# Main attention of a two-layer block: square turns on VectorE, 32-row products of the values in two pieces, each head weighed by itself

## The chip, the cores and the metric

One core of a Trainium2 chip runs the whole program in one launch. The metric is device time in microseconds (us). All matrix work runs on the TensorE into PSUM, which has eight banks of 128 partitions x 512 float32. VectorE (DVE in the rows), ScalarE (ACT) and GpSimd (POOL) do the rest, and SyncE (SP) issues most DMAs.

## The reference, cut to what matters

Two transformer layers over 1024 tokens of width 256. The change lies in the first layer's main attention: 16 heads, queries and keys of 192 columns (128 plain, 64 rotated), values that come from 64 latent columns.

```
qf = concat([q_nope, q_pe], -1);  kf = concat([k_nope, k_pe], -1)
scores = einsum('bhqd,bhkd->bhqk', qf, kf) * scale
probs  = softmax(scores)                    # 1024 x 1024 for each of 16 heads
ctx    = einsum('bhqk,bhkd->bhqd', probs, v)
main_out = ctx @ o_w.T
out = gates[..., 0:1] * main_out + gates[..., 1:2] * pattern_out
```

Beside it stand a second ("pattern") attention, whose stage comes first, a mixture of experts, and in the second layer a causal attention and another mixture of experts. They are not touched.

## The kernel before, in words

The weights are folded so that a head's keys and queries are 128 columns wide (64 latent, 64 rotated) and the values of all heads are the same 64 latent columns `kvx`; the head's value and output weights are folded into `mo` (256 columns for each pair of heads).

Main attention is cut into 32 units. Unit u is a pair of heads (u // 4) and 256 queries (u % 4), and has four score blocks i of 128 queries x 1024 keys: head i % 2, query half i // 2. One block takes these steps:

- `pe_score` (L1850 to L1852): six TensorE products of 512 columns (three split products for each half of the keys) into one of two bank pairs, `wide[0]` and `wide[1]` (banks 0 to 3). The two pairs alternate, so block n waits for the exponential of block n - 2.
- `dve_score` (L1859): VectorE takes the negated row maximum of 1024 columns.
- `act_expo` (L1874): ScalarE takes the exponential into `Pq`, of which there are eight, with the row sums as an accumulator.

The values need the keys on the partitions. `pe_transposed` (L1883) turns the four blocks of a unit with TensorE, four 128x128 squares into one bank for each of eight key tiles k; `act_copy` (L1896) copies six of the eight tiles to SBUF and `dve_copy` (L1901) the two in `BY_VECTOR`. `pe_pvm` (L1951) then makes the products of the values: for each k and each head one of 128 rows (keys), 64 weight columns and 256 moving columns. Head 0 goes to partitions 0 to 63 of bank 6, head 1 to 64 to 127.

Meanwhile `dve_recip` takes the reciprocals of the row sums, times the gate, and turns them in a small square turn (L1917); `sp_shares` and `sp_spread` carry them by DMA through HBM to `Rs`. `dve_weigh` (L1962) multiplies bank 6 by `Rs` into `OTm` in one operation, `pe_project_out` (L1974) multiplies by `mo`, and `dve_add_out` (L1988) adds to x.

Every pair's queries and keys are prepared beside the pair before it: `pe_prep` (L1604; six products, four `rope` and two `lat`), `act_product` (L1637, the copy), `sp_swap` (four DMAs that swap halves for the rotation) and `pool_product` (L1659 to L1685, GpSimd: cosine, sine, sum, cast, subtraction). The copy of product k waits for the swap and the cosine product of k - 1, or for its low part when that one was a `lat`.

The order of work is written out by hand in `main_order`; every engine runs its own steps of that list in order. In unit u stand the scores and exponentials of unit u + 1, the eight turns of unit u with their copies, and the values, weighing, projection and addition of unit u - 1. One preparation product stands every fifth turn. The banks 4, 5 and 7 go around among turns, projections and preparation products (`PTB`).

Of the kernel before, what the change touches and what calls it, by code (L numbers as in the profile page):

```python
# [62 lines left out]
PREP_EVERY = 5  # L63

BY_VECTOR = (0, 6)


def up(x, half, m):
# [6 lines left out]
    (28, 7): [("temperature",), ("wup", 0), ("wdown", 0)],  # L75
    (30, 6): [("stats", 0)],
    (31, 2): [("normed", 0)],
    (31, 5): [("turn", 0), ("hT", 0)],
    (31, 7): [("wup", 1), ("wdown", 1)],
    (31, "values"): [("logits", 0)],  # L80
}


def main_order():

    order = [("expo", 0, 1), ("score", 0, 2), ("score", 0, 3), ("ctx", 0), ("ctx", 1), ("expo", 0, 2), ("cadd", 0),  # L90
             ("ctx", 2), ("expo", 0, 3), ("cadd", 1), ("ctx", 3), ("cadd", 2), ("cadd", 3)]
    chunks = []

    def turn(u, k):
        order.extend([("t", u, k), ("copy", u, k)])
        if chunks:
            order.extend(chunks.pop(0))
        order.extend(BESIDE_LAST.get((u, k), ()))

    def score(u, i):  # L100
        if u < 32:
            order.append(("score", u, i))

    def expo(u, i):
        if u < 32:
            order.append(("expo", u, i))

    def output(u):
        order.extend([("project", u), ("add", u)])

    for u in range(32):
        if u % 4 == 0 and u // 4 + 1 < 8:
            for i in range(len(FIRST)):
                chunks.extend([[("prep", u // 4 + 1, i), ("pcopy", u // 4 + 1, i)]] + [[]] * (PREP_EVERY - 1))
        score(u + 1, 0)
        turn(u, 0)
        order.append(("rec", u))
        score(u + 1, 1)
        expo(u + 1, 0)
        turn(u, 1)  # L120
        if u:
            order.extend([("pv", u - 1), ("ot", u - 1)])
        expo(u + 1, 1)
        turn(u, 2)
        score(u + 1, 2)
        turn(u, 3)
        if u:
            output(u - 1)
        expo(u + 1, 2)
        turn(u, 4)  # L130
        order.append(("spread", u))
        score(u + 1, 3)
        turn(u, 5)
        turn(u, 6)
        expo(u + 1, 3)
        turn(u, 7)
    assert not chunks
    order.extend([("pv", 31)] + BESIDE_LAST[31, "values"] + [("ot", 31)])
    output(31)
    return order  # L140

# [196 lines left out]
def program(nc, a, out):  # L338
# [27 lines left out]
    bank = [wide[i // 2][:, i % 2, :] for i in range(4)] + [nc.alloc_psum_tensor(f"bank{i}", [128, 512], F32)[:] for i in range(4, 8)]  # L366
# [128 lines left out]
    Pq = [MP.sb("Pq0", [128, T], F32)]  # L495
    Pt = [sb("Pt0", [128, 512], F32, at=W0A), sb("Pt1", [128, 512], F32, at=HN)]
    M1 = Region(S0 + 64 * 1024)
    Pq += [M1.sb(f"Pq{i}", [128, T], F32) for i in range(1, 7)]
    Pt += [M1.sb("Pt2", [128, 512], F32), MP.sb("Pt3", [128, 512], F32)]
    M1 = Region(HTP)  # L500
    Pq += [M1.sb("Pq7", [128, T], F32)]
    Pt += [M1.sb(f"Pt{i}", [128, 512], F32) for i in range(4, 10)]
    Pql = Pq[:7] + [sb("Pq7l", [128, T], F32, at=WKPE + 4096)]
    Ptl = Pt[:4] + [sb(f"Pt{i}l", [128, 512], F32, at=(KV + 2048 * (i - 4) if i < 8 else WKPE + 2048 * (i - 8)))
                    for i in range(4, 10)]
# [736 lines left out]
    mp_ok, tr_mm, ev_v, clear_ok = (sem(n) for n in ("mp_ok", "tr_mm", "ev_v", "clear_ok"))  # L1242
# [383 lines left out]
    def act_product(e, p, k):  # L1626
# [10 lines left out]
        e.activation(t12[:, 0, :], bank[PTB["prep", p, k][0] if p else BANK_P0[k][0]][:], ACT.Copy).then_inc(pc_ok, 1)  # L1637
# [156 lines left out]
    pta_ok, ptv_ok = sem("pta_ok"), sem("ptv_ok")  # L1794
    d_shares, d_spread = sem("d_shares"), sem("d_spread")
    for s_ in MAIN:
        if s_[0] == "score":
            slot_ = s_[2] % 2 if s_[1] == 0 else 1 - s_[2] % 2
# [3 lines left out]
    PTB, PTC = {}, {}  # L1802
    free_, copies_ = [(cadd_ok, 3), (op_cT, 4), (cadd_ok, 4)], [0, 0]
    for s_ in MAIN:
        if s_[0] in ("t", "project", "prep"):
            b_ = len(PTB) % 3
            PTB[s_] = ((4, 5, 7)[b_], free_[b_])
            if s_[0] == "project":
                free_[b_] = (add_ok, s_[1] + 1)
            elif s_[0] == "prep":  # L1810
                free_[b_] = (pc_ok, len(FIRST) * s_[1] + s_[2] + 1)
            else:
                v_ = s_[2] in BY_VECTOR
                copies_[v_] += 1
                PTC[s_[1:]] = ((pta_ok, ptv_ok)[v_], copies_[v_])
                free_[b_] = PTC[s_[1:]]
# [5 lines left out]
    def probabilities(u, i):  # L1822
        n = 4 * u + i
        return (Pql if u >= 30 else Pq)[n % 8]
# [1476 lines left out]
```

## Time and profile before

| | |
|---|---|
| time, median of 3 runs | 1294.52 us (1292.11 to 1296.56) |
| the profiled execution | 1291.33 us, its span 1289.5 us |
| busy share of the span | PE 96%, DVE 60%, ACT 57%, POOL 41% |
| mean granted TensorE clock | 0.992 |
| turns on TensorE (L1883) | 1024 of 128x128 |
| products of the values (L1951) | 512, in 1024 records |

In the profile a float32 product leaves two records, so that one unit's sixteen products of the values show as x32; a turn, and a product of the split type, leaves one. The duration of a record on PE holds its way through the array, so records that follow each other overlap; what a product costs is the distance from start to start. PEld is the load of the weights, which runs beside the products. The main attention runs from about 265 us to about 770 us of the span.

### The profile page before, as it was taken

What the parts mean: (1) busy time and instruction counts of PE and PEld (TensorE: products, weight loads), DVE (VectorE), ACT (ScalarE), POOL (GpSimd) and SP (SyncE); (2) the same over time, 40 slices, a digit from 0 to 9 for tenths busy, and PEclk for the clock granted to TensorE, in tenths of its full rate; (3) what the DMA queues carried; (4) which work ended last, traced back from release to release, by engine and by line L of the source; (5) the groups of instructions that cost most, each with busy time, mean ns of one, the idle gap of its engine ahead of it and who ended that gap; (6) DMA issues with size and microseconds to landing.
All of it is one profiled execution on the core that took longest, in us unless ns stands there. A gap on an engine that the chain in (4) does not pass through costs nothing.

```text
span 1289.5 us, 22502 instructions
## 1 busy us (share of the span) xinstructions
PE 1243.0 (96%) x8298; PEld 875.0 (68%) x8298; DVE 768.3 (60%) x1254; ACT 732.9 (57%) x1370; POOL 533.4 (41%) x531
## 2 busy tenths in 40 slices
PE   8999999999999999999999998999998998999997
PEld 5544334477777777777777777889753444678997
DVE  4689978245454444445454666555667763855555
ACT  3479978855555555555555635332355676435553
POOL 5266274248576666767666124443100000512211
PEclk9999999999999999999999999999999999989999
DMA  7780000001101011111111021020233310101111
GB/s 287 200 180 2 2 19 11 10 18 29 38 22 38 22 38 27 32 32 32 29 36 54 25 72 76 27 72 12 74 74 88 72 38 1 34 17 33 50 42 34
DMA packets 40887, 64.44 MB, mean 50 GB/s; under 512 B 8221, under 2 KB 27421, under 8 KB 39837
## 3 DMA queue, kind: packets, MB, share of 16 engines
q1 hardware_dynamic: 40776, 62.99, 17.8%
q8 instruction: 67, 1.10, 0.4%
q14 instruction: 44, 0.35, 0.1%
HBM read 45.60 MB, written 8.45 MB: 42 GB/s over the span
## 4 chain that ended last, share of the span: by engine, by line
PE 85%; DVE 8%; ACT 3%; issue 2%; DMA 1%; POOL 1%; SPq 0%; ACTq 0%; DVEq 0%; POOLq 0%
PE bank L1951 9%; PE bank L1883 9%; PE bank L1513 8%; PE bank L2151 6%; PE bank L2152 6%; PE bank L2153 6%; PE bank L1604 5%; PE bank L1850 5%; PE bank L1852 5%; PE bank L1851 5%; PE bank L1470 4%; PE bank L1333 3%; PE bank L1974 2%; PE bank L1450 2%; DVE mpc L1412 2%
## 5 line engine op out<-in xcount | busy, mean ns | idle before, releaser
L1859 DVE TENSOR_REDUCE nmq<-bank 128x1 f32<-128x1024 f32 x128 | 155.8, 1217 | 151.8 <-PE bank L1852 151.8
L1491 ACT ACTIVATE Pb<-bank 128x512 f32<-128x512 f32 (+3 forms) x355 | 180.6, 573 | 30.2 <-PE bank L1470 9.3
L1896 ACT ACTIVATE Pt<-bank 128x512 f32<-128x512 f32 x187 | 110.7, 594 | 118.8 <-PE bank L1883 117.9
L1874 ACT ACTIVATE Pq<-bank,nmq 128x1024 f32<-128x1024 f32 x127 | 141.7, 1116 | 58.7 <-DVE nmq L1859 58.7
L1341 DVE TENSOR_REDUCE mp<-bank 128x2 f32<-128x1024 f32 x128 | 153.5, 1221 | 27.5 <-PE bank L1333 26.7
L1883 PE MATMUL bank<-idf,Pq 128*128 128x128 f32 x1016 | 145.7, 275 | 1.4 <-ACT Pq7l L1874 1.2
L1883 PEld LDWEIGHTS bank<-idf,Pq 128*128 128x128 f32 x1016 | 119.1, 140 | 36.5 <-issue 11.9
L1412 DVE TENSOR_REDUCE mpc<-bank 128x2 f32<-128x1024 f32 (+2 forms) x96 | 88.4, 953 | 46.3 <-PE bank L1400 23.2
L1951 PE MATMUL bank<-Pt,kvx 128*64 128x256 f32 x992 | 114.1, 382 | 0.0
L1850 PE MATMUL bank<-qk1h,qk0h 128*128 128x512 f32 x256 | 109.4, 427 | 0.4 <-ACT Pq L1874 0.4
L1513 PE MATMUL bank<-Pb,vx 128*17 128x256 f32 (+3 forms) x1222 | 106.3, 407 | 0.7 <-ACT OTa L1527 0.5
L1852 PE MATMUL bank<-qk1h,qk0l 128*128 128x512 f32 x256 | 100.8, 394 | 0.0
L1851 PE MATMUL bank<-qk1l,qk0h 128*128 128x512 f32 x256 | 100.0, 391 | 0.0
L1951 PEld LDWEIGHTS bank<-Pt,kvx 128*64 128x64 f32 x992 | 68.6, 137 | 37.7 <-issue 6.6
L2126 POOL TENSOR_TENSOR cTt<-cTt,gab 128x256 f32<-128x256 f32 x8 | 6.1, 760 | 181.9 <-DVE cTt L2121 181.6
L2353 POOL TENSOR_TENSOR hl<-hf,hh 128x512 fp32r<-128x512 f32 x32 | 41.8, 1307 | 83.8 <-ACT hh L2340 83.8
L1661 POOL TENSOR_TENSOR t<-t,sinT 128x512 f32<-128x512 f32 x32 | 40.9, 1278 | 74.7 <-DMA t<-t 74.5
L1470 PE MATMUL bank<-qstr,kstr 64*128 64x512 f32 x256 | 70.9, 494 | 0.6 <-ACT Pb L1491 0.6
L2567 POOL TENSOR_TENSOR v1l<-wr,v1h 128x512 fp32r<-128x512 f32 x25 | 32.1, 1288 | 95.0 <-ACT v1h L2562 95.0
L1470 PEld LDWEIGHTS bank<-qstr,kstr 64*128 64x128 f32 x256 | 28.2, 183 | 56.8 <-ACT Pb L1491 36.2
L1659 POOL TENSOR_TENSOR Rt<-t,cosT 128x512 f32<-128x512 f32 x32 | 41.1, 1285 | 60.0 <-ACT t L1637 58.5
L1450 PE MATMUL bank<-qst,kst 107*128 107x512 bf16 (+3 forms) x192 | 54.3, 333 | 7.8 <-ACT qst L1437 3.5
(374 smaller groups left out, 2951.7 us busy)
## 6 DMA issues: line engine op xcount, KB each, us to landing
t<-t SPq DMA_DIRECT2D x128, 64.0 KB, 2.0
wr<-wf SPq DMA_DIRECT2D x25, 256.0 KB, 2.6
wraw<-wf SPq DMA_DIRECT2D x8, 768.0 KB, 4.6
scratch<-stgr SPq DMA_DIRECT2D x4, 1024.0 KB, 4.0
Rs<-shares SPq DMA_DIRECT2D x64, 64.0 KB, 2.7
scratch<-stg SPq DMA_DIRECT2D x8, 384.0 KB, 2.6
qst<-scratch SPq DMA_DIRECT2D x9, 256.0 KB, 8.4
owT<-owT SPq DMA_DIRECT2D x1, 2048.0 KB, 11.2
```

Source lines behind the costliest of these rows:

```text
L1341: e.tensor_reduce(mp[:, w % 3, :, j, kh], wide[slot][:], AX, ALU.max).then_inc(ring_ok, 1)
L1412: e.tensor_reduce(mpc[:, w // 2 % 3, a0:a0 + 2, j, kh], wide[slot][:, :, 0:c], AX, ALU.max).then_inc(ring_ok, 1)
L1470: e.matmul(bank[b][:], kst2[r, hp, kt * 128:kt * 128 + 128], qst2[r, hp, cols(half)], start=True, stop=True).then_inc(st_mm[0], 1)
L1491: e.activation(PBR[l][i % len(PBR[l])][:, 0:c], bank[b][:, 0:c], ACT.Exp, scale=0.25).then_inc(exp_ok[0], 1)
L1513: last = e.matmul(bank[6][32 * a:32 * a + 17, to:to + c], vx[:, t, h * 17:h * 17 + 17], PBR[l][i % len(PBR[l])][:, q0:q0 + c], start=(t == ...
L1850: e.matmul(o, qh[:, qs], kh[:, ks], start=True, stop=False)
L1851: e.matmul(o, qh[:, qs], kl[:, ks], start=False, stop=False)
L1852: last = e.matmul(o, ql[:, qs], kh[:, ks], start=False, stop=True)
L1859: e.tensor_reduce(nmq[:, n % 8:n % 8 + 1], scores(u, i), AX, ALU.max, negate=True).then_inc(mp_ok, 1)
L1874: e.activation(probabilities(u, i)[:], scores(u, i), ACT.Exp, bias=nmq[:, n % 8:n % 8 + 1], accum_out=sums[:, u % 2, i:i + 1]).then_inc(ex ...
L1883: last = e.transpose(bank[b][:, 128 * c:128 * c + 128], probabilities(u, 2 * (c % 2) + c // 2)[:, 128 * k:128 * k + 128], idf[:])
L1951: last = e.matmul(bank[6][64 * hd:64 * hd + 64, 0:256], kvx[:, k, :], transposed(u, k)[:, 256 * hd:256 * hd + 256], start=(k < 1), stop=(k ...
```

## The change

- *Turns.* `pe_transposed`, `act_copy` and `dve_copy` are gone. `dve_turn` lets VectorE transpose one score block of 128x1024, in 32x32 squares, from one of three `P` buffers (before: eight `Pq`) into `PT[u % 2]`, a tile of 32 key blocks x 128 columns. After it, key 32 b + r of a query block stands at row r of the row group its queries were in: rows 32 g to 32 g + 31 of `PT` hold 32 keys for the queries of row group g, and the 128 columns are two query halves of two heads, 32 each. The exponential of block n waits for the turn of block n - 3.
- *Values.* `sp_values` lays the values out four times, once, with sixteen DMAs: `kv4[s]` has keys 32 s to 32 s + 31 of every 128 in each of the four row groups. `pe_pvm` makes 32 x 4 products of 32 rows, 64 weight columns and 128 moving columns, row group g into bank 4 + g, in two pieces of 16 key blocks: `("pv", u, 0)` and `("pv", u, 1)`. The four banks are one PSUM tensor `rest`.
- *Weighing.* `dve_weigh` runs once for each head, over partitions 0 to 63 of the four banks, and writes the head's half of `OTm`.
- *Banks.* The projection always goes to bank 7 and preparation products to 5 and 6 in turn, which the values use as well. So the values of a unit wait for the addition of the unit before and for ScalarE's copies of all preparation products ahead of them (`COPIED`), and a preparation product for the last weighing ahead of it and for the copy before the last.
- *Order.* `main_order` is written anew: in unit u the values of u - 1 stand in two pieces, after score blocks 2 and 3; the projection of u - 2 after score block 0; preparation products at places `PREP_AT`, counted in score blocks. The steps for the experts beside the last units stand at other places.

```diff
+PREP_AT = ((4, 5, 8, 9, 12, 13), (0, 1, 4, 8, 9, 12))
...
+    preps = {16 * (p - 1) + at: (p, i) for p in range(1, 8) for i, at in enumerate(PREP_AT[p > 1])}
...
+    for u in range(1, 32):
+        order.append(("score", u, 0))
+        output(u - 2)
+        prep(4 * u)
+        order.extend([("rec", u - 1), ("vturn", u - 1, 3), ("expo", u, 0)])
+        order.extend(BESIDE_LAST.get((u, 0), ()))
+        order.append(("score", u, 1))
+        prep(4 * u + 1)
+        order.extend([("spread", u - 1), ("vturn", u, 0), ("expo", u, 1)])
+        order.extend(BESIDE_LAST.get((u, 1), ()))
+        order.extend([("score", u, 2), ("pv", u - 1, 0), ("vturn", u, 1), ("expo", u, 2)])
+        order.extend([("score", u, 3), ("pv", u - 1, 1), ("ot", u - 1), ("expo", u, 3), ("vturn", u, 2)])
+    output(30)
+    order.extend([("rec", 31), ("vturn", 31, 3), ("turn", 0), ("spread", 31), ("pv", 31, 0), ("pv", 31, 1), ("hT", 0),
+                  ("wup", 1), ("wdown", 1), ("ot", 31), ("project", 31), ("logits", 0), ("add", 31)])
...
+    def dve_turn(e, u, i):
+
+        c, n = 64 * (i % 2) + 32 * (i // 2), 4 * u + i
+        e.wait_ge(exp_ok[1], n + 1)
+        if i == 0 and u >= 2:
+            e.wait_ge(pv_mm[1], u - 1)
+        elif i == 0:
+            e.wait_ge(*((pv_mm[0], 128), (op_mm, 4))[u])
+        source = probabilities(u, i)[:].rearrange("p (b k) -> p b k", k=32)
+        if u < 31:
+            e.transpose(PT[u % 2][:, :, c:c + 32], source).then_inc(pt_ok, 1)
...
+    def sp_values(e):
+
+        e.wait_ge(sh_mm, 16)
+        e.wait_ge(pv_mm[0], 128)
+        for s in range(4):
+            for g in range(4):
+                e.dma_start(kv4[s][32 * g:32 * g + 32, :, :], kvx[32 * s:32 * s + 32, :, :]).then_inc(d_kv, 16)
...
-    def pe_pvm(e, u):
...
-        for k in range(NT):
-            for hd in range(2):
-                last = e.matmul(bank[6][64 * hd:64 * hd + 64, 0:256], kvx[:, k, :],
-                                transposed(u, k)[:, 256 * hd:256 * hd + 256],
-                                start=(k < 1), stop=(k == NT - 1), skip_group_check=True)
-        last.then_inc(pv_mm[1], 1)
+    def pe_pvm(e, u, part):
+
+        if part == 0:
+            if u:
+                e.wait_ge(ot_ok[1], u)
+                e.wait_ge(add_ok, u)
...
+            e.wait_ge(*COPIED[u])
+            e.wait_ge(pt_ok, 4 * u + 4)
+        for b in range(16 * part, 16 * part + 16):
+            for g in range(4):
+                rows = slice(32 * g, 32 * g + 32)
+                last = e.matmul(rest[0:64, g, 0:128], kv4[b % 4][rows, b // 4, :], transposed(u, b)[rows, :],
+                                start=(b == 0), stop=(b == 31), skip_group_check=True)
+        if part:
+            last.then_inc(pv_mm[1], 1)
...
-        e.tensor_tensor(OTm[:], bank[6][:, 0:256], Rs[:, u % 2, :], ALU.mult).then_inc(ot_ok[1], 1)
+        by_row = "p (j g q) -> p j g q"
+        for hd in range(2):
+            rows = slice(64 * hd, 64 * hd + 64)
+            last = e.tensor_tensor(OTm[rows, :].rearrange(by_row, j=2, g=4),
+                                   rest[0:64, :, 64 * hd:64 * hd + 64].rearrange("p g (j q) -> p j g q", j=2),
+                                   Rs[rows, u % 2, :].rearrange(by_row, j=2, g=4), ALU.mult)
+        last.then_inc(ot_ok[1], 1)
```

## Rows read from the trace of the kernel before

**Rows 1.** The page: busy time of each engine, and the chain by engine.
```profile
PE 1243.0 (96%) x8298; PEld 875.0 (68%) x8298; DVE 768.3 (60%) x1254; ACT 732.9 (57%) x1370; POOL 533.4 (41%) x531
...
PE 85%; DVE 8%; ACT 3%; issue 2%; DMA 1%; POOL 1%; SPq 0%; ACTq 0%; DVEq 0%; POOLq 0%
```

**Rows 2.** Busy time by stretch: us, PE, PEld, DVE, ACT, POOL, clock, DMA.
```profile
265.00:770.70 505.70, 502.84 (x3238) 393.58 (x3239) 259.61 (x388) 284.89 (x496) 301.24 (x300) 1.00 0.12 32
319.50:693.20 373.70, 373.70 (x2403) 291.67 (x2401) 185.00 (x265) 213.19 (x372) 247.81 (x251) 1.00 0.12 30
693.20:735.60 42.40, 42.40 (x285) 32.77 (x283) 24.01 (x37) 26.11 (x46) 12.91 (x11) 1.00 0.18 54
735.60:770.70 35.10, 32.49 (x233) 24.98 (x231) 22.26 (x50) 16.20 (x27) 7.09 (x6) 1.00 0.12 35
```

**Rows 3.** Timeline (start, duration in us), VectorE: the weighing of three units.
```profile
639.69 0.42 DVE L1962 TENSOR_TENSOR OTm<-bank,Rs 128x256 f32<-128x256 f32 x1 [3.63 <-PE bank L1951]
...
701.99 0.42 DVE L1962 TENSOR_TENSOR OTm<-bank,Rs 128x256 f32<-128x256 f32 x1 [3.65 <-PE bank L1951]
...
715.74 0.42 DVE L1962 TENSOR_TENSOR OTm<-bank,Rs 128x256 f32<-128x256 f32 x1 [2.51 <-PE bank L1951]
```

**Rows 4.** Timeline of 702 to 716 us, TensorE: one unit.
```profile
702.28 0.48 PE L1850 MATMUL bank<-qk1h,qk0h 128*128 128x512 f32 x1
702.60 0.39 PE L1851 MATMUL bank<-qk1l,qk0h 128*128 128x512 f32 x1
702.83 0.39 PE L1852 MATMUL bank<-qk1h,qk0l 128*128 128x512 f32 x1
...
704.19 1.03 PE L1974 MATMUL bank<-mo,OTm 128*128 128x256 f32 x4
...
706.88 1.47 PE L1883 MATMUL bank<-idf,Pq 128*128 128x128 f32 x12
...
712.01 3.67 PE L1951 MATMUL bank<-Pt,kvx 128*64 128x256 f32 x32
...
715.62 0.66 PE L1883 MATMUL bank<-idf,Pq 128*128 128x128 f32 x4
```

**Rows 5.** Timeline, TensorE: products in four column groups, 256 and 128 columns.
```profile
260.77 1.06 PE L1513 MATMUL bank<-Pb,vx 128*17 128x256 f32 x16
...
1015.57 0.27 PE L1513 MATMUL bank<-Pbc,vx 128*17 128x128 f32 x1
...
1015.67 0.27 PE L1513 MATMUL bank<-Pbc,vx 128*17 128x128 f32 x1
```

**Rows 6.** Timeline, TensorE: loads and products in two row groups.
```profile
191.84 0.19 PEld L1470 LDWEIGHTS bank<-qstr,kstr 64*128 64x128 f32 x2 [0.42 <-issue]
191.84 0.50 PE L1470 MATMUL bank<-qstr,kstr 64*128 64x512 f32 x2
```

**Rows 7.** Groups by line and shape: busy us, mean ns of one; idle before.
```profile
L1859 DVE TENSOR_REDUCE nmq<-bank 128x1 f32<-128x1024 f32 x128 | 155.8, 1217 | 151.8 <-PE bank L1852 151.8
L1988 DVE TENSOR_TENSOR x<-x,bank 128x512 f32<-128x512 f32 x32 | 22.0, 688 | 5.3 <-PE bank L1974 3.0
L1962 DVE TENSOR_TENSOR OTm<-bank,Rs 128x256 f32<-128x256 f32 x32 | 13.6, 424 | 80.7 <-PE bank L1951 80.5
L1917 DVE STREAM_TRANSPOSE rrow<-rsum 128x32 f32<-128x32 f32 x32 | 6.8, 212 | 1.1
...
L1874 ACT ACTIVATE Pq<-bank,nmq 128x1024 f32<-128x1024 f32 x127 | 141.7, 1116 | 58.7 <-DVE nmq L1859 58.7
...
L1850 PEld LDWEIGHTS bank<-qk1h,qk0h 128*128 128x128 f32 x256 | 48.2, 188 | 8.0 <-ACT Pq L1874 0.7 <-issue 0.5
L1951 PEld LDWEIGHTS bank<-Pt,kvx 128*64 128x64 f32 x992 | 68.6, 137 | 37.7 <-issue 6.6
```

**Rows 8.** Timeline: GpSimd's subtraction, a product's copy, its second GpSimd product.
```profile
692.88 2.64 POOL L1685 TENSOR_TENSOR qk0l<-t,qk0h 64x512 fp32r<-64x512 f32 x2
698.38 0.60 ACT L1637 ACTIVATE t<-bank 128x512 f32<-128x512 f32 x1 [0.54 <-PE bank L1604]
...
703.43 1.28 POOL L1661 TENSOR_TENSOR t<-t,sinT 128x512 f32<-128x512 f32 x1 [3.04 <-DMA t<-t]
```

More of the change, by code:

```diff
@@ L74 @@
 BESIDE_LAST = {
[L75 to L80, printed above, removed]
+    (29, 0): [("temperature",), ("wup", 0), ("wdown", 0)],
+    (31, 0): [("stats", 0)],
+    (31, 1): [("normed", 0)],
 }
+PREP_AT = ((4, 5, 8, 9, 12, 13), (0, 1, 4, 8, 9, 12))
 def main_order():
-    order = [("expo", 0, 1), ("score", 0, 2), ("score", 0, 3), ("ctx", 0), ("ctx", 1), ("expo", 0, 2), ("cadd", 0),
-             ("ctx", 2), ("expo", 0, 3), ("cadd", 1), ("ctx", 3), ("cadd", 2), ("cadd", 3)]
@@ L92, in main_order @@
[L92 to L106, printed above, removed]
-    def output(u):
[L109 to L136, printed above, removed]
@@ L137, in main_order, with prep @@
-    assert not chunks
-    order.extend([("pv", 31)] + BESIDE_LAST[31, "values"] + [("ot", 31)])
-    output(31)
+    order = [("expo", 0, 1), ("score", 0, 2), ("ctx", 0), ("ctx", 1), ("vturn", 0, 0), ("expo", 0, 2), ("score", 0, 3),
+             ("cadd", 0), ("ctx", 2), ("vturn", 0, 1), ("cadd", 1), ("expo", 0, 3), ("ctx", 3), ("cadd", 2), ("vturn", 0, 2),
+             ("cadd", 3)]
+    preps = {16 * (p - 1) + at: (p, i) for p in range(1, 8) for i, at in enumerate(PREP_AT[p > 1])}
+    def prep(n):
+        if n in preps:
+            order.extend([("prep", *preps[n]), ("pcopy", *preps[n])])
@@ new lines, in output @@
+    def output(u):
+        if u >= 0:
+            order.extend([("project", u), ("add", u)])
+    for u in range(1, 32):
[10 more added lines that the diff above has]
+        order.extend([("score", u, 3), ("pv", u - 1, 1), ("ot", u - 1), ("expo", u, 3), ("vturn", u, 2)])
@@ L365, in program @@
     wide = [nc.alloc_psum_tensor(f"bank{2 * i}", [128, 2, 512], F32) for i in range(2)]
-    bank = [wide[i // 2][:, i % 2, :] for i in range(4)] + [nc.alloc_psum_tensor(f"bank{i}", [128, 512], F32)[:] for i in range(4, 8)]
+    rest = nc.alloc_psum_tensor("bank4", [128, 4, 512], F32)
+    bank = [wide[i // 2][:, i % 2, :] for i in range(4)] + [rest[:, i, :] for i in range(4)]
     x = sb("x", [128, NT, D], F32)
@@ L1636, in act_product @@
                 e.wait_ge(lt_lo, done)
-        e.activation(t12[:, 0, :], bank[PTB["prep", p, k][0] if p else BANK_P0[k][0]][:], ACT.Copy).then_inc(pc_ok, 1)
+        e.activation(t12[:, 0, :], bank[PREP[p, k][0] if p else BANK_P0[k][0]][:], ACT.Copy).then_inc(pc_ok, 1)
     def sp_swap(e, p, k):
@@ L1797, in program @@
         if s_[0] == "score":
-            slot_ = s_[2] % 2 if s_[1] == 0 else 1 - s_[2] % 2
+            slot_ = s_[2] % 2
             SCORE[s_[1:]] = (slot_, score_free[slot_])
             score_free[slot_] = (exp_ok[1], 4 * s_[1] + s_[2] + 1)
-    PTB, PTC = {}, {}
-    free_, copies_ = [(cadd_ok, 3), (op_cT, 4), (cadd_ok, 4)], [0, 0]
+    PREP, COPIED, weighed_, copied_ = {}, {}, 0, len(FIRST)
     for s_ in MAIN:
[L1805 to L1816, printed above, removed]
+        if s_[0] == "prep":
+            PREP[s_[1:]] = (5 + len(PREP) % 2, (ot_ok[1], weighed_) if weighed_ else (op_cT, 4))
+            copied_ += 1
+        elif s_[0] == "ot":
+            weighed_ += 1
+        elif s_[0] == "pv":
+            COPIED.setdefault(s_[1], (pc_ok, copied_))
     def tiles_of(h):
@@ L1973, in pe_project_out @@
         for q in range(2):
-            last = e.matmul(bank[b][:, 256 * q:256 * q + 256], OTm[:, 128 * q:128 * q + 128], mo[:, u // 4, :],
+            last = e.matmul(bank[7][:, 256 * q:256 * q + 256], OTm[:, 128 * q:128 * q + 128], mo[:, u // 4, :],
                             start=True, stop=True)
@@ L1978, in dve_add_out @@
     def dve_add_out(e, u):
-        b, _ = PTB["project", u]
         e.wait_ge(pr_mm, u + 1)
@@ L2970, in scalar @@
                 act_expo(e, s[1], s[2])
-            elif s[0] == "copy":
-                act_copy(e, s[1], s[2])
             elif s[0] == "pcopy":
```

91 lines of the change are left out of this document (27 added, 64 removed).

## The prediction

> **What bounds the kernel now.** I read the page first: the TensorE is busy for 96% of the span and carries 85% of the chain that ended last [rows 1]. Then the busy times by stretch, cut at the first score product of units 4, 28 and 31: in the stretch 319.5 to 693.2 us the TensorE is busy for all of its 373.7 us, VectorE for 185.0 and ScalarE for 213.2, at a granted clock of 1.00, its higher level of 2.4 GHz [rows 2]. So main attention is bound by the TensorE's order of work, and what VectorE and ScalarE do is hidden. The times at which VectorE weighs a unit (a unit is two heads by 256 queries) give the period: 62.3 us from 639.69 to 701.99 for four units with their six preparation products, 13.75 us for a unit without any [rows 3].
>
> The timeline then prices a unit on the TensorE [rows 4]. A score product of 512 columns starts 0.23 us after the one before it and 0.32 us after work of another kind; a score block of six takes 1.39 us, plus 0.09 at such an entry. Twelve turns take 1.47 us, less 0.27 for the last one's own duration: 0.109 us each, 3.5 us for a unit's 32. The values take 3.61 us from their first record to the next turn. The projection's four records (0.217 apart) take 0.87 us.
>
> **The change, part by part.**
>
> *Turns.* 32 TensorE turns go (3.5 us a unit), with the short entries around their eight groups. ScalarE loses six copies and VectorE two, which nobody waited for. VectorE gets four turns of 128x1024 in squares. No row shows that shape. The square turn of 128x32 takes 0.212 us and the 1024-column maximum 1.217 [rows 7]. Lower end: a fixed 0.15 and a column per 0.96 GHz cycle, as the maximum's, 1.2 us. Upper end: 32 times the small one, 6.8 us. I take 1.24 (the small one and 992 columns more at the maximum's rate), since the small one's 32 columns cost it next to nothing. VectorE then has 4 x 1.22 + 4 x 1.24 + 0.84 (two weighings at the 0.424 of the old one, an estimate: half the partitions, as many columns) + 0.69 + 0.6 (reciprocal, gate and small turn at the 0.2 of the last) = 12.0 us a unit: below the TensorE's, but no longer loose. At 2.3 us a turn my schedule grows by 22 us, so this matters only beyond about 2 us. One 0.424 more for the weighing costs 3.
>
> *The values.* Before, 16 products of 256 columns, two side by side: 32 records in 3.61 us. Now 128 products of 128 columns with 32 rows, four row groups side by side: 256 records, in two pieces of 128. What a round of four costs is shown only for four column groups: 16 records of 256 columns in 1.06 us, less 0.38 of the last, is 0.22 a round; two records of one 128-column product start 0.10 apart [rows 5]. With 0.109 a round, a piece is 32 x 0.109 + 0.05 at its entry = 3.55 us. Two row groups do run side by side, loads too: two loads of 128 columns, 0.19 us each, end within 0.19 us together [rows 6]. So the two pieces take 7.1 us in place of 3.6: only 64 of the 128 columns of the array are used. The 3.5 us that the turns gave are spent. Bounds for a piece: 3.5 us below; above, if weight loads of four row groups follow one another. A 64-column load is 137 ns, a 128-column one 188 [rows 7], so 64 columns cost about 0.053; four are 0.21 a round, 6.8 us a piece.
>
> *TensorE sum of a unit without preparation:* four score blocks 5.56 + three entries 0.27 + projection 0.92 with its entry + two pieces with an entry each 7.28 = 14.03 us, against 13.75 measured. The change has no gain on the engine that bounds.
>
> *New waits.* The order is now score 0, project, (prep), score 1, (prep), score 2, piece 1, score 3, piece 2. From the start of score 0, with VectorE's queue in its order: weighing 0.2 to 1.1 (it waited for the last piece, and the turn of the previous unit's block 2 waited behind it), that turn to 2.3, maximum 0 to 3.5, addition, reciprocals, turn, and so on; ScalarE's exponential of 1.116 and its 0.19 read [rows 7] end at 4.9. Score 2 needs that bank pair: the TensorE is ready at 3.9 and waits 1.0. The unit is 15.06, +1.31.
> With preparation: piece 1 writes banks 4 to 7 and so waits for ScalarE's copy of each product before it. The copy of the second rope product waits for GpSimd and the swap DMAs of the first: 4.45 us from the copy's end to the second GpSimd product [rows 8]. The first copy ends at 4.6, the second at 9.8, the TensorE is ready at 8.1 and idles 1.8: the unit takes 14.03 + 2 x 1.39 + 1.8 = 18.6. For the latent pair the second copy waits for cast and subtraction (2.64 us the latter [rows 8]): 14.03 + 2 x 1.16 + 1.44 = 17.8. Units with one product: 14.03 + 1.39 + 0.68 (exponential 0 stands behind the copy) = 16.1, twice. Four units: 68.6 against 62.3, where the old order has no such wait.
> Sixteen DMAs spread the values over the row groups, once, on SP, ahead of the first unit's shares. Four score blocks and the context products (over 20 us) lie between what they wait for and the first piece: nothing; without that cover some microseconds, once.
>
> *Sum.* Units 4 to 27: 6 x 68.6 = 411.5 against 373.7, +37.8. Units 28 to 30: 45.2 against 42.4 [rows 2], +2.8. Start: before, 54.5 us from the third score block to unit 4 (505.7 less the three stretches of [rows 2]); now 64.7 (four heavier units, one unit's values more done by then, context products as before), +10. Tail: 35.1 us before; now one piece fewer is left, but the last turn and 2.9 us of waiting stand open (partly filled by hidden-state turns), some 31.4: -3.7. Together +47 us. The profiled execution took 1291.33 us (span 1289.5); so 1338. The median of the three runs is 3 us above it: 1341. I say 1340.
>
> A rule of the Trainium skill speaks further against the change. "TensorE: Matmul & The Clock Gate", Part 3, gives 3.07 times, not four, for four row groups of 32 rows at 512 columns. By it a round would be 0.142 us, an estimate, a piece 4.6, and the time 1407. Rows 5 show full overlap for column groups; none here shows it for four row groups.
>
> **The rivals.**
> *A. The pieces cannot be fed.* 128 loads and 128 products in 3.55 us is one instruction per 14 ns. The densest long stretch shown is 32 records with their 32 loads in 3.61 us, 56 ns each [rows 4], or 16 and 16 in about 0.9, 27 ns [rows 5], both set by columns, so neither is a limit. If 27 ns were one, a piece would be 6.9 us; with serial loads 6.8. That is +3.3 x 64 = +210: 1550. It decides from 3.7 us a piece on, each 0.1 costing 6.4 us.
> "Runtime: NRT & Kernel Launch", Instruction fetch mechanics, has such a rule: the sequencer needs about 20 cycles per instruction. At the 1.2 GHz that the TensorE page gives it this is 16.7 ns, 4.27 us a piece (estimates), and 1386 us. No run here shows it.
> *B. The waits close.* If maxima, copies and turns come earlier than I place them, only TensorE work is left: 14.03 x 4 + 4 x 1.39 + 2 x 1.16 = 64.0 per four units, +1.7 x 7, with start and tail +15: 1309. Against it: both waits have margins over 0.6 us the wrong way.
> *C. Faster.* One mechanism: first and second record of a product run side by side too, so that a piece is 1.8 us. The TensorE sum falls to 10.5, the unit to 13.0 with VectorE near its bound, 61.7 per four: -9 in all, 1285. It decides below about 2.0 us a piece. Against it: those records start 0.10 apart at 128 columns and 0.22 at 256 [rows 5], a round after each other.
> *D. The squares' turns cost over 2 us:* 1362 at 2.3, part of the range.
>
> **How the numbers follow.** Forecast 1340 (own range 1322 to 1365) 0.52; A 0.30 (1365 to 1550, more of it low); B 0.10; C 0.06; 0.02 for a change below 0.3%, some 4 us, which is about what a measurement of this kernel can tell from none. Splitting edges: faster 0.07, same 0.03, slower 0.90. Leaving out C and A above 1450: 1308 to 1450.
>
> **What would show it.** Right: records of a piece in fours, 0.109 apart from four to four, a piece 3.5 to 3.6 us; TensorE idle about 1 us before score 2 and 1.4 to 1.8 before piece 1 where two products stand, released by ScalarE's copy; periods 15.1 and 68.6; square turns 1.2 us; stages outside 265 to 770 us unchanged. Wrong: a piece over 3.7 us (A), a TensorE without gaps (B), a piece under 2 us (C), VectorE without idle time (D).

## The result, and the profile after

The changed kernel takes 1344.76 us (median of 4 runs, 1343.73 to 1349.51), the kernel before 1293.32 beside it (1288.22 to 1296.56): 1.0409 times as long, 95% interval 1.0366 to 1.0452, or 51 us more. Forecast were 1340 and a range of 1308 to 1450.

The page of the kernel after: busy time of each engine, the instruction queue's DMAs (packets, MB), the chain by engine, as in [rows 1].
```profile
PE 1263.1 (94%) x14433; PEld 923.6 (69%) x14436; DVE 882.4 (66%) x1354; ACT 625.2 (47%) x1178; POOL 531.6 (40%) x531
...
q8 instruction: 115, 1.88, 0.6%
...
PE 74%; DVE 10%; ACT 5%; issue 4%; POOL 3%; DMA 2%; SPq 1%; ACTq 0%; POOLq 0%; DVEq 0%
```
TensorE is busy 20 us longer, with 14433 records in place of 8298; VectorE has 114 us more and ScalarE 108 less. The fetch of instructions moved 115 packets in place of 67.

Busy time by stretch of the kernel after (columns as in [rows 2]), cut at the same score blocks: the whole of main attention, units 4 to 27, units 28 to 30, tail.
```profile
265.61:823.55 557.94, 522.07 (x9365) 439.51 (x9365) 374.07 (x488) 177.35 (x304) 299.70 (x300) 0.99 0.13 34
331.21:745.15 413.94, 389.83 (x7012) 327.05 (x7008) 271.77 (x336) 131.99 (x228) 249.00 (x253) 1.00 0.11 29
745.15:790.57 45.42, 43.17 (x857) 35.99 (x853) 34.80 (x45) 15.93 (x26) 3.18 (x2) 1.00 0.16 46
790.57:823.55 32.98, 28.32 (x569) 24.97 (x565) 25.87 (x57) 7.89 (x12) 7.14 (x6) 0.90 0.17 56
```
Against [rows 2], where the TensorE was busy for all 373.70 us of units 4 to 27, it is now busy for 389.83 and idle for 24. So of the 40.2 us that these units cost more, 16 are work and 24 are new idle time. The stages outside main attention take 1.5 us more in the profiled execution (0.6 ahead of it, 0.9 behind).

Groups of the kernel after (busy us, mean ns of one, idle before and its releasers): the values' products, the maxima (L1859 in [rows 7]), the square turns and the weighing (L1962 there).
```profile
L1908 PE MATMUL bank<-PT,kv 32*64 32x128 f32 x7936 | 233.3, 270 | 24.2 <-ACT t L1600 24.0
...
L1814 DVE TENSOR_REDUCE nmq<-bank 128x1 f32<-128x1024 f32 x128 | 153.4, 1199 | 89.9 <-PE bank L1807 89.8
...
L1842 DVE STREAM_TRANSPOSE PT<-P 128x1024 f32<-128x1024 f32 x124 | 152.2, 1227 | 17.3 <-ACT P L1829 16.3
...
L1922 DVE TENSOR_TENSOR OTm<-bank,Rs 64x256 f32<-64x256 f32 x64 | 26.7, 417 | 80.3 <-PE bank L1908 74.0
```
The timeline of the TensorE after, in a unit without preparation (start, duration, what; the bracket is the idle time before it and its releaser), to be read beside [rows 4]:
```profile
749.81 0.50 PE L1805 MATMUL bank<-qk1h,qk0h 128*128 128x512 f32 x1 [0.75 <-ACT P L1829]
...
751.41 3.72 PE L1908 MATMUL bank<-PT,kv 32*64 32x128 f32 x128
...
756.64 3.72 PE L1908 MATMUL bank<-PT,kv 32*64 32x128 f32 x128
```
and in a unit with two rotated products (here of the keys, `kmh`), in one with two latent products (`lth`), and in one with one rotated product:
```profile
541.01 0.58 PE L1566 MATMUL bank<-kmh,wkh 128*128 128x512 f32 x1
...
548.34 3.72 PE L1908 MATMUL bank<-PT,kv 32*64 32x128 f32 x128 [1.40 <-ACT t L1600]
...
575.31 0.58 PE L1566 MATMUL bank<-qah,lth 128*128 128x512 f32 x1
...
582.53 4.10 PE L1908 MATMUL bank<-PT,kv 32*64 32x128 f32 x128 [1.78 <-ACT t L1600]
...
593.98 0.58 PE L1566 MATMUL bank<-qah,wqh 128*128 128x512 f32 x1
...
597.27 0.50 PE L1805 MATMUL bank<-qk1h,qk0h 128*128 128x512 f32 x1 [0.39 <-ACT P L1829]
```
The reader is to see two things: a piece is 128 records in 3.72 us (3.46 from first start to last, a round of four every 0.109), and the TensorE stands idle before score 2 and before piece 1, where nothing stood idle before.

### The profile page after: what moved, and what is told of

Read it like the earlier page. It is cut to its first block, busy times and chain, and to the rows that moved or that the text cites. A ratio compares the mean times of both kernels' runs of the same rounds, so it can differ in the third digit from the quotient of the medians.

```text
span 1343.2 us, 34497 instructions
## 1 busy us (share of the span) xinstructions
PE 1263.1 (94%) x14433; PEld 923.6 (69%) x14436; DVE 882.4 (66%) x1354; ACT 625.2 (47%) x1178; POOL 531.6 (40%) x531
## 2 busy tenths in 40 slices
DMA packets 41699, 66.25 MB, mean 49 GB/s; under 512 B 8476, under 2 KB 27676, under 8 KB 40604
## 4 chain that ended last, share of the span: by engine, by line
PE 74%; DVE 10%; ACT 5%; issue 4%; POOL 3%; DMA 2%; SPq 1%; ACTq 0%; POOLq 0%; DVEq 0%
PE bank L1908 17%; PE bank L1475 7%; PE bank L2109 6%; PE bank L2111 5%; PE bank L2110 5%; PE bank L1432 4%; PE bank L1805 4%; PE bank L1566 3%; PE bank L1807 3%; PE bank L1806 3%; PE bank L1295 2%; PE bank L1933 2%; DVE mpc L1374 2%; PE bank L1412 2%; PE bank L1362 1%
## 5 line engine op out<-in xcount | busy, mean ns | idle before, releaser
L1908 PE MATMUL bank<-PT,kv 32*64 32x128 f32 x7936 | 233.3, 270 | 24.2 <-ACT t L1600 24.0
L1908 PEld LDWEIGHTS bank<-PT,kv 32*64 32x64 f32 x7936 | 218.3, 133 | 47.6 <-issue 47.6
L1829 ACT ACTIVATE P<-bank,nmq 128x1024 f32<-128x1024 f32 x128 | 142.2, 1113 | 186.1 <-DVE nmq L1814 186.1
L1842 DVE STREAM_TRANSPOSE PT<-P 128x1024 f32<-128x1024 f32 x124 | 152.2, 1227 | 17.3 <-ACT P L1829 16.3
L1374 DVE TENSOR_REDUCE mpc<-bank 128x2 f32<-128x1024 f32 (+2 forms) x96 | 88.3, 953 | 43.3 <-PE bank L1362 22.2
L1600 ACT ACTIVATE t<-bank 128x512 f32<-128x512 f32 x48 | 28.7, 598 | 183.8 <-PE bank L1566 138.3
L1922 DVE TENSOR_TENSOR OTm<-bank,Rs 64x256 f32<-64x256 f32 x64 | 26.7, 417 | 80.3 <-PE bank L1908 74.0
L1805 PEld LDWEIGHTS bank<-qk1h,qk0h 128*128 128x128 f32 x256 | 48.0, 187 | 33.9 <-ACT P L1829 15.5
```

What stands on the lines that cost most here:

```text
L1374: e.tensor_reduce(mpc[:, w // 2 % 3, a0:a0 + 2, j, kh], wide[slot][:, :, 0:c], AX, ALU.max).then_inc(ring_ok, 1)
L1805: e.matmul(o, qh[:, qs], kh[:, ks], start=True, stop=False)
L1829: e.activation(probabilities(u, i)[:], scores(u, i), ACT.Exp, bias=nmq[:, n % 8:n % 8 + 1], accum_out=sums[:, u % 2, i:i + 1]).then_inc(ex ...
L1842: e.transpose(PT[u % 2][:, :, c:c + 32], source).then_inc(pt_ok, 1)
L1908: last = e.matmul(rest[0:64, g, 0:128], kv4[b % 4][rows, b // 4, :], transposed(u, b)[rows, :], start=(b == 0), stop=(b == 31), skip_group ...
```

## The experiments

Each kernel ran beside the kernel before, on the same chip; ratios are to that one. "Over four units" is a sixth of the time from the first score of unit 4 to that of unit 28: 68.99 us in the changed kernel.

**Is a piece array work, or as long as its instructions take? (e1_half)** Odd key blocks go to the other half of the columns, with the same number of instructions. Their sums are not read, so this kernel leaves out half of the keys.
```diff
-                last = e.matmul(rest[0:64, g, 0:128], kv4[b % 4][rows, b // 4, :], transposed(u, b)[rows, :],
-                                start=(b == 0), stop=(b == 31), skip_group_check=True)
+                part_ = slice(64 * (b % 2), 64 * (b % 2) + 64)
+                last = e.matmul(rest[part_, g, 0:128], kv4[b % 4][rows, b // 4, :], transposed(u, b)[rows, :],
+                                start=(b < 2), stop=(b >= 30), skip_group_check=True)
```


> Leaves out half of the keys in the values: the products of the odd key blocks go to PSUM partitions 64-127 of the same four banks, and only partitions 0-63 are weighed. The number of instructions is the same (256 loads and 256 products per unit); only the place in the array is other, so that eight tiles (four row groups by two column halves) can work beside each other instead of four. Theory (a piece of 3.46 us is array work, four products of 128 columns beside each other per round of 0.109 us): a piece takes about 1.75 us, a unit without products of the preparation goes from 15.14 to about 12-13 us (VectorE's 12.0 us per unit is then near), four units from 68.9 to about 61-63, so some 45 to 60 us off: 1285 to 1300. Rival 1 (a piece is as long as 128 loads and 128 products take to be supplied, 13.5 ns each): the piece stays at 3.4-3.5 us and the time within 5 us of 1345. Rival 2 (VectorE or ScalarE bounds the unit as closely as TensorE): the piece halves, but the unit falls by under 1 us and the kernel by under 25.

1294.28 us, ratio 1.0021 [0.9999, 1.0043]; 62.4 over four units. The timeline of this kernel, two pieces:
```profile
555.44 2.05 PE L1909 MATMUL bank<-PT,kv 32*64 32x128 f32 x125 [1.83 <-ACT t L1600]
...
559.15 0.43 PE L1909 MATMUL bank<-PT,kv 32*64 32x128 f32 x3 [1.66 <-issue]
...
585.62 2.12 PE L1909 MATMUL bank<-PT,kv 32*64 32x128 f32 x128 [1.36 <-ACT t L1600]
```
The same 128 records and 128 loads take 1.83 us from first start to last: 7 ns per instruction. So 3.46 was array work, and the 50 us that come back are nearly the whole loss of the change. 64 pieces, each 1.63 us shorter, would be 104 us; new waits take much of the rest: between 400 and 700 us the TensorE waits 10.5 us for the weighing and 10.0 for nothing that the profile names, beside 15.0 for ScalarE's copy, which is still there. The first piece above shows something new: after 125 records the TensorE stands still for 1.66 us, and no semaphore held it ("issue").

**The two waits (e2_copies, e3_order, e4_both)**
```diff
+    t1b = sb("t1b", [128, 512], F32, at=KVT)
+    def copied_to(p, k):
+        return t1b[:] if p and k % 2 else t12[:, 0, :]
...
-        e.activation(t12[:, 0, :], bank[PREP[p, k][0] if p else BANK_P0[k][0]][:], ACT.Copy).then_inc(pc_ok, 1)
+        e.activation(copied_to(p, k), bank[PREP[p, k][0] if p else BANK_P0[k][0]][:], ACT.Copy).then_inc(pc_ok, 1)
```


> From pair 1 on, the copies of every other product of the preparation go to a second buffer, so that ScalarE's copy waits for GpSimd's work on the product before the last and not on the last one. Theory (TensorE's idle time before piece 1, 1.8-1.9 us with a rotated product and 1.35 with a latent one, is the wait for that copy): the idle time before piece 1 is gone or under 0.6, units with two products go from 18.4 to about 17, four units from 68.9 to about 66, some 19 us off: 1320 to 1332. Rival (the copy is late because ScalarE is late with the exponential of block 2 or 3, behind VectorE's turns): the idle time stays, the time is within 4 us of 1345.

1324.46 us, ratio 1.0253 [1.0228, 1.0277]; 66.25 over four units. 20 us came back. Longest waits of the TensorE from 400 to 700 us in this kernel (us in total, times, longest):
```profile
PE bank L1821 <- ACT P L1845: 3.6, 9, 0.4
PE bank L1949 <- DVE OTm L1938: 3.1, 4, 1.6
PE bank L1924 <- issue: 0.4, 1, 0.4
```
The wait of the values for a copy is gone from the list; in the changed kernel it leads with 14.4 us, 9 times.

```diff
-        order.append(("score", u, 0))
+        order.extend([("score", u, 0)] + [("vturn", u - 1, 2)] * (u > 1) + [("vturn", u - 1, 3)])
         output(u - 2)
         prep(4 * u)
-        order.extend([("rec", u - 1), ("vturn", u - 1, 3), ("expo", u, 0)])
+        order.extend([("rec", u - 1), ("expo", u, 0)])
...
-        order.extend([("score", u, 3), ("pv", u - 1, 1), ("ot", u - 1), ("expo", u, 3), ("vturn", u, 2)])
+        order.extend([("score", u, 3), ("pv", u - 1, 1), ("ot", u - 1), ("expo", u, 3)])
```


> VectorE's order alone: the maximum of block 0 goes ahead of the turn of block 2 of the unit before, and the turns of blocks 2 and 3 go ahead of the addition and the reciprocals. Theory (before score 2 TensorE waits 0.75 us for the exponential of block 0, whose maximum stands behind a turn): that wait shrinks to under 0.2, but values piece 0 and the addition of the output are then later on VectorE, so that most comes back as a wait before piece 1: 0 to 4 us faster, 1341 to 1345. Rival 1 (nothing takes its place): 0.75 x 11 units without products and 0.39 x 13 others = 13 us off, 1332. Rival 2 (VectorE's two turns in a row hold the exponential of block 0, which waits for its P buffer): slower by over 5 us.

1344.64 us, ratio 1.0403 [1.0378, 1.0428]: no change. Units without preparation go from 15.14 to 14.89 us, but one of the three takes 16.33: there the wait moved. In units 4 to 27 it was not touched: 4.7 us in 12 waits before score 2, as in the changed kernel, so the expected shrinking to under 0.2 did not come. With the second buffer:

> The second buffer for the copies and VectorE's other order together. Theory (two separate waits, the first worth 19 us and the second little, because it moves): 19 to 23 us off, 1322 to 1326, at most 3 us better than the second buffer alone. Rival (the two waits stand in one another's way, and together they free what neither does alone): over 8 us better than the sum of the two runs.

1327.96 us, ratio 1.0266 [1.0237, 1.0294], not told apart from the second buffer alone. This change of VectorE's order does not remove the wait before score 2, alone or with the buffer.

**The order as a whole (o1_order)**
```diff
+        order.extend([("rec", u - 1), ("score", u, 0), ("vturn", u - 1, 3)])
+        prep(4 * u)
+        order.extend([("expo", u, 0), ("score", u, 1), ("vturn", u, 0), ("expo", u, 1), ("spread", u - 1)])
+        prep(4 * u + 1)
+        output(u - 2)
...
+        order.extend([("score", u, 2), ("vturn", u, 1), ("expo", u, 2), ("score", u, 3), ("pv", u - 1, 0), ("pv", u - 1, 1), ("expo", u, 3), ("vturn", u, 2), ("ot", u - 1)])
```


> The changed kernel in another order inside a unit, nothing else. TensorE: score 0, first product, score 1, second product, projection, scores 2 and 3, both pieces of the values one after the other. VectorE: reciprocals ahead of the maximum of block 0, the turn of block 3 of the unit before behind it, then a maximum and a turn in turns, the weighing last. Theory (two waits, 0.39-0.75 us before score 2 and 1.3-1.9 us before piece 1, come from what stands between; with both pieces behind score 3 the copies have over 7 us of scores to cover them): both idle times under 0.5 us, four units from 68.9 to 64-66 us, 20 to 26 us off: 1319 to 1325, as much as the second buffer gave (1324.5). Rival (each wait only moves, to the scores of the next unit, whose exponentials are then late): within 8 us of 1345.

1311.53 us, ratio 1.0138 [1.0114, 1.0161]; 63.9 over four units. 33 us less by order alone, more than expected: the start gave some 4 us too. That is close to 62.3, the old kernel's period [rows 3], and to the 64.0 that the prediction had for the array's work alone (its case B). Still it is 1.4% slower than before: with nearly all waits gone (5.0 us left in units 4 to 27) the change loses.

**Eight tiles with nothing left out (f1_full, f2_full_order)**
```diff
+            last = e.tensor_tensor(OTm[:, hd, :].rearrange(by_row, j=2, g=4),
+                                   rest[:, :, 64 * hd:64 * hd + 64].rearrange("p g (j q) -> p j g q", j=2),
+                                   Rs[:, hd, :].rearrange(by_row, j=2, g=4), ALU.mult)
...
+            for hd in range(2):
+                last = e.matmul(bank[7][:, 256 * q:256 * q + 256], OTm[:, hd, 128 * q:128 * q + 128],
+                                mo2[:, u // 4 % 2, hd, :], start=(hd == 0), stop=(hd == 1))
```


> The values in eight tiles with nothing left out: even key blocks to PSUM partitions 0-63, odd ones to 64-127, each head weighed on all 128 partitions, and the projection, four products instead of two, adds the two halves over its 128 rows with the output weights of a head held twice. The order is that of the changed kernel. Theory (the piece of 1.8 us stays, the projection costs 0.9 us of TensorE more): 5 to 15 us over the kernel with half of the keys (1294), so 1299 to 1309. Rival 1 (the shares, now spread over 128 partitions into a single buffer after the weighing, come late and hold the weighing and with it the next projection): over 1320. Rival 2 (the projection's extra products hide in TensorE's idle time before piece 1): 1292 to 1296.

1347.56 us, ratio 1.0411 [1.0376, 1.0446]: the first rival. From 400 to 700 us in this kernel, a wait of VectorE, and the TensorE's for it:
```profile
DVE OTm L1936 <- DMA Rs<-shares: 47.2, 12, 5.4
```
```profile
PE bank L1948 <- DVE OTm L1936: 27.0, 12, 3.6
```
Twelve weighings wait for their shares, up to 5.4 us, and the projections behind them 27.0 us in all, against 10.5 in e1_half. The single buffer for the shares (two before, now that a head's shares stand on all partitions) and the projection's 0.9 us cost what the halved pieces gave; the two were not run apart.

> The eight-tile kernel of the run before in the other order of o1_order. Theory (with pieces of 1.8 us the array's sum per unit is about 11.0 us without and 13.7 us with products, VectorE's 12.0; only the waits on copies and exponentials kept it from these in the first order): four units 54 to 57 us against 68.9 in the changed kernel and 62.3 before, and the kernel at 1250 to 1268, faster than the kernel before. Rival (VectorE, GpSimd's products of 3 to 5 us each or the swaps by DMA bound a pair from below, at about 60 us per four units): 1280 to 1295, the order gives under 15 us here.

1282.40 us, ratio 0.9916 [0.989, 0.9943]; 59.2 over four units (58.7 in the expectations below). Faster than before, but not by what was expected, and the rival's engines are not the reason. The timeline and the waits of the TensorE (400 to 700 us) in this kernel:
```profile
572.96 3.36 PE L1920 MATMUL bank<-PT,kv 32*64 32x128 f32 x218
577.55 0.91 PE L1920 MATMUL bank<-PT,kv 32*64 32x128 f32 x38 [1.22 <-issue]
```
```profile
PE bank L1920 <- issue: 26.7, 20, 2.8
PE bank L1564 <- issue: 0.4, 1, 0.4
PE bank L1803 <- ACT P L1827: 0.3, 1, 0.3
```
The waits for other engines are gone (0.3 us in 300). What stands in their place is a standstill in the middle of the values, 20 times, on nothing that the profile shows. In the trace's list of DMA packets the instruction queue's have 16 KB each; between 200 and 820 us there are 82 here, 78 in the changed kernel and 33 in the one before, and the nearest two are 3.30, 3.40 and 12.99 us apart.

The place of the standstills tells more. Count all records of the TensorE in the order of the trace (products, loads and those of its sequencer). Every standstill of over 0.4 us within the values, 29 between 200 and 830 us here, 8 in f3_spaced, 8 in e1_half, 6 in f1_full and 2 in o1_order, has a number of records ahead of it that leaves the remainder 193 when divided by 256, while the waits for other engines in the same kernels stand at all kinds of remainders. And each standstill ends 2.2 to 3.3 us after the start of the latest 16 KB packet, 1.2 to 1.6 after its end. In the timeline above the packet ran from 575.11 to 576.19, and the TensorE went on at 577.55. So a packet is 256 instructions, and the TensorE stands still at the seam between two of them.

**Is that standstill the supply of instructions? (x1_half_blocks, f3_spaced)** Both edits are against f2_full_order. The first kernel leaves out the second half of the key blocks.
```diff
-        for b in range(16 * part, 16 * part + 16):
+        for b in range(8 * part, 8 * part + 8):
...
-                part_ = slice(64 * (b % 2), 64 * (b % 2) + 64)
+                part_ = slice(64 * part, 64 * part + 64)
...
-                                start=(b < 2), stop=(b >= 30), skip_group_check=True)
+                                start=(b % 8 == 0), stop=(b % 8 == 7), skip_group_check=True)
```


> f2_full_order without half of the key blocks (the values leave out half of the keys): blocks 0 to 7 go to PSUM partitions 0-63, blocks 8 to 15 to 64-127, one after the other. So four tiles work beside each other instead of eight, on half of the products: the array needs as long as before, 3.5 us per unit, with 256 instead of 512 load and product instructions. Theory (the gaps of 0.9 to 2.8 us inside the values of f2_full_order, 26.7 us in 300 us, are waits for instructions: the blocks of 16 KB, 256 instructions, came at least 3.3 us apart, and 512 instructions at 6.9 ns each are through in 3.5): the gaps are gone, four units go from 58.7 to 53.5-55, 25 to 32 us off: 1250 to 1258. Rival (the gaps are the array's or the operands', such as PSUM banks written by two column groups or VectorE's turns writing the buffer beside them): gaps of the first kind go too, but then pieces show a slower pace and not a standstill; gaps of the second kind stay, and the time is within 8 us of 1282.

1236.50 us, ratio 0.956 [0.9528, 0.9591]; 52.8 over four units. The values of a unit in this kernel:
```profile
571.94 3.36 PE L1920 MATMUL bank<-PT,kv 32*64 32x128 f32 x128 [0.73 <-ACT t L1598]
...
583.85 3.36 PE L1920 MATMUL bank<-PT,kv 32*64 32x128 f32 x128
```
With half the instructions and nearly the same need of the array the standstills are gone: the TensorE's waits from 400 to 700 us name no "issue" any more. The 46 us are more than the 25 to 32 expected. In the profiled executions 38 of them lie in units 4 to 27, where 28.2 us of standstills are gone. The two pieces, which now fill different halves of the columns, also overlap at their seam: a unit's values take 3.10 us from first start to last, where f2_full_order needs 3.66 (its 128 records take 1.83) and, with its standstills and slower rounds, 5.14 on average. That is 49 us in 24 units, of which some 12 come back as waits for other engines. The other 8 us lie outside these units, most of them in units 28 to 30 (35.2 us against 43.3), which had 5.2 us of standstills. This run also keeps four tiles at work instead of eight, so by itself it doesn't tell the supply from the array; f3_spaced keeps the eight.

> f2_full_order with one thing else: score 3 stands between the two pieces of the values, and the projection ahead of the second product. Nothing is left out. Theory (waits for instructions, blocks at least 3.3 us apart): score 3 gives the fetch 1.4 us in which only 12 instructions are used, so about half of the 1.3 us per unit comes back: four units 56 us against 58.7, 8 to 18 us off, 1264 to 1275. Rival (score 3 later makes its exponential late, and with it the turn that the next values wait for): 1280 to 1295.


```diff
-        order.extend([("expo", u, 0), ("score", u, 1), ("vturn", u, 0), ("expo", u, 1), ("spread", u - 1)])
-        prep(4 * u + 1)
+        order.extend([("expo", u, 0), ("score", u, 1), ("spread", u - 1)])
...
+        prep(4 * u + 1)
-        order.extend([("score", u, 2), ("vturn", u, 1), ("expo", u, 2), ("score", u, 3), ("pv", u - 1, 0), ("pv", u - 1, 1), ("expo", u, 3), ("vturn", u, 2), ("ot", u - 1)])
+        order.extend([("expo", u, 1), ("vturn", u, 0), ("score", u, 2), ("vturn", u, 1), ("expo", u, 2), ("pv", u - 1, 0), ("score", u, 3), ("pv", u - 1, 1), ("expo", u, 3), ("vturn", u, 2), ("ot", u - 1)])
```
The edit moves a little more than the expectation says: ScalarE's second copy also goes ahead of exponential 1, and VectorE's addition ahead of turn 0.

1273.31 us (6 runs), ratio 0.9832 [0.9794, 0.987]; 57.7 over four units. Its waits of the TensorE, 400 to 700 us:
```profile
PE bank L1920 <- issue: 8.3, 8, 2.7
PE bank L1920 <- ACT t L1598: 4.6, 6, 1.3
```
With the twelve instructions of a score block between two pieces of 256 the standstills fall from 26.7 to 8.3 us, with the same products in the same eight tiles; 4.6 come back as a wait for the copy. The small moves on ScalarE and VectorE were not run alone, but no standstill waited for either engine. This is the best version that leaves nothing out: 20 us under the kernel before, 71 under the changed one.

**The fall of the clock (t1_filled)**
The changed kernel's granted clock was 0.50 (1.2 GHz) twice in main attention. Stretches of it (columns as in [rows 2], the clock third from the end), the second just behind the first, the third in the tail:
```profile
375.50:378.50 3.00, 3.00 (x64) 3.00 (x61) 1.25 (x1) 1.32 (x4) 2.78 (x4) 0.50 0.05 16
378.90:382.00 3.10, 3.10 (x65) 2.38 (x61) 0.01 (x1) 0.00 (x0) 0.33 (x1) 1.00 0.02 5
...
809.00:815.50 6.50, 5.56 (x84) 5.19 (x86) 6.43 (x12) 1.65 (x3) 3.30 (x3) 0.50 0.04 12
```
Before the first fall the TensorE had waited 1.9 us for a copy, before the second 2.0 us for the weighing of unit 30. Its longest wait, 2.15 us at 445 us, had no fall behind it.
```diff
+                if s[1] == 30:
+                    e.wait_ge(exp_ok[1], 127)
+                    for _ in range(4):
+                        e.matmul(bank[0][:, 0:256], idf[:], kvT[:, 0:256], start=True, stop=True)
```


> The changed kernel with four products of 256 columns whose result nobody reads, in TensorE's idle gap of 2.0 us at 805.8 us ahead of the projection of unit 30. Theory (the granted clock fell from 2.4 to 1.2 GHz at 808.8 us because TensorE had been idle just before): the clock stays at 2.4 GHz there, the 256 products of the last values take 7.0-7.4 us instead of 8.96, and the time falls by 1 to 3 us. Rival (the fall has another cause, such as the transposes of full width behind the projection): it stays where it was, or follows the gap of 0.9 us at 811.5 us, and the time is the same.

1346.32 us (6 runs), ratio 1.0419 [1.0386, 1.0451]: the whole can't tell 2 us. The profile can; the tail of this kernel by stretch and its last values:
```profile
806.00:830.00 24.00, 21.18 (x412) 18.96 (x405) 16.68 (x36) 6.33 (x10) 7.14 (x6) 1.00 0.35 114
```
```profile
814.33 7.36 PE L1908 MATMUL bank<-PTl,kv 32*64 32x128 f32 x256 [1.71 <-DVE PTl L1845]
```
The clock stays at 2.4 GHz there, the last values take 7.09 us from first start to last instead of 8.96, and the tail 31.1 instead of 33.0: the size that the theory gave. The cause is not settled by it, since e3_order kept a gap of 2.1 us at the same place and its clock did not fall. What all eleven profiles of these kernels say together, between 250 and 820 us: of 37 falls 34 came within an idle gap of the TensorE of 1.8 to 6.2 us or up to 1.4 us behind it, but other gaps, up to 3.3 us long, had no fall. So most falls go with such a gap, and many gaps have none.

## Why the prediction was right

**The turns.** VectorE's square turn took 1.227 us where 1.24 were taken from bounds of 1.2 and 6.8. The lower end was right: it runs at the maximum's pace per column. The weighing took 0.417, the addition 0.672. VectorE's work, 12.0 us a unit by the forecast and 11.6 in units 28 to 30, did not bind; case D is out.

**The values.** The step that decided, and it was right in size: a round of four row groups 0.109 us, a piece 3.46 from start to start and 3.65 to the next score product, against 3.55 and its entry of 0.09. The sum of the array's work was nearly right: units without preparation took 15.14 us with 0.75 idle in them, so 14.39 of work, where 14.03 was forecast. That the unit came out within 0.1 us (15.06 forecast) is in part luck: the work was 0.36 too short, the wait 0.25 too long. The pieces were right (3.65 each with the entry, 7.30 for 7.28). The four score blocks with their entries took 1.50, 1.74, 1.60 and 1.58 us (the second less its idle 0.75) where 5.83 was the sum: 0.59 more; the projection took 0.67, 0.25 less than the 0.92.

**The rule of the Trainium skill.** "TensorE: Matmul & The Clock Gate", Part 3, has 3.07 times for four row groups of 32 rows at 512 columns. By it rounds would be 0.142 us, an estimate. The trace differs: 0.109 held over whole pieces, at 128 columns. The measurement decides.

**The waits.** Both at their place and with the releaser named. Before score 2, 1.0 forecast and 0.75 measured, 0.39 with one product (0.68 forecast). Before piece 1 the sum was right and the two terms were not, in units 4 to 27: with two rotated products 1.8 was forecast and 1.33 to 1.40 measured, with two latent ones 1.44 forecast and 1.77 to 1.90 measured, once 2.15. The errors of some 0.4 us cancel, which is luck. The copies of a rotated pair:
```profile
542.82 0.60 ACT L1600 ACTIVATE t<-bank 128x512 f32<-128x512 f32 x1 [5.06 <-PE bank L1566]
...
547.45 1.27 POOL L1624 TENSOR_TENSOR t<-t,sinT 128x512 f32<-128x512 f32 x1 [2.60 <-DMA t<-t]
547.48 0.60 ACT L1600 ACTIVATE t<-bank 128x512 f32<-128x512 f32 x1 [2.97 <-DMA t<-t]
```
The term that was too long is the 4.45 us from the copy's end to the second GpSimd product, taken from the kernel before: here it is 4.03. In a latent pair the second copy ended 9.14 us after the start of its unit, about where the terms put it, and the values started 0.25 us after that end, which the sum did not have. My terms, 1.8 and 1.44 once in each of seven pairs, come to 23 us, the measured waits for a copy to 24.0; taking their cause away with a buffer gave 20. Case B, the waits close, is out for the changed kernel, but o1_order reached it by order alone: 1311.5, where B had 1309.

**The sum.** Start 65.6 (64.7 forecast), units 4 to 27 413.9 (411.5), units 28 to 30 45.4 (45.2), tail 33.0 (31.4): +52.2 in the profiled execution against +47.1. The 5 us missing are 1.7 and 1.9 of the clock at 1.2 GHz (the unit at 375 us took 20.04 instead of 18.3, and the tail's values 1.9 longer), and small entries.

**Case A, and why it was priced wrongly.** The pieces could be fed, so A did not happen, but its two prices were both wrong. 27 ns per instruction as a floor is far off: the densest runs have 7 ns. Nor do loads of four row groups follow one another. What limits is not an instruction but the block: 256 instructions are fetched at a time, and no two blocks come nearer than 3.2 to 3.5 us in any of the changed kernels (3.24 in e1_half, 3.50 in f1_full). A piece of the changed kernel is 256 instructions in 3.5 us, so it stood just at the edge. Two of its pieces show it: they take 3.91 and 3.83 us instead of 3.46, each with a step of 0.2 to 0.5 us at the same remainder, 193, and 2.3 us after the start of a packet. The eight-tile kernels, where a block is used up in 1.8 us, fell over it. The Trainium skill, "Runtime: NRT & Kernel Launch", Instruction fetch mechanics, says that instructions come in blocks of 16 KiB, the next fetched while the present one runs: the trace agrees, with packets of 16 KB. The same section of the Trainium skill takes the fetch to be hidden behind a floor of about 20 cycles per instruction. The runs differ on both, with 7 ns from start to start and 26.7 us of standstill in 300. That the standstill is the fetch is shown by its place, only at a seam of 256 records and just behind a packet, and by two runs that change the number and the spacing of instructions; how many blocks are held ready was not measured.

**Case C** had a wrong mechanism (first and second record of a product beside each other do not occur) and a right number: a piece of 1.83 us by other means, with half of the keys left out, gave 1294, where C had 1285.

## What to carry to other kernels

A product of 32 rows and 64 columns fills one of eight tiles: four row groups alone use half of the array, so count the tiles at work before counting what the removed work saves. Price a new order by its new waits: here 24 of 40 us were waits, and reordering one list gave 33 us back. Count instructions as well as array time where products are small: 512 in a row stood still twice in the whole of main attention at 13.6 ns each (o1_order) and in nearly every unit at 7 ns (f2_full_order), and a few long products between two runs of 256 took most of that away.

## What the runs showed of the hardware that I had not expected

- Eight tiles of 32x64 work beside each other: 128 loads and 128 products of 128 columns in 1.83 us, 7 ns per instruction.
- Blocks of 256 instructions come 3.2 to 3.5 us apart at the nearest, and a stretch of more than 256 at 7 ns each can stand still, for 0.4 to 2.8 us, always at the seam of two blocks.
- A stretch of 3.4 to 6.8 us, once 10.2, at 1.2 GHz goes with some, not all, of the TensorE's idle gaps of 2 us and more within otherwise full work; a piece in it took 5.12 us instead of 3.46. A wait of 2 us can so cost 1.7 to 1.9 us again behind it.
